# Late part of the second dense pass of a four-layer graph network: slots a block ahead, early sums added by TensorE, tables between root and norm, and the last set of blocks split

## The chip, the cores and the metric

The kernel runs on one core of a Trainium2 chip. The metric is the device time of one execution in microseconds (us). TensorE's clock has two levels, 1.2 and 2.4 GHz; the profile shows the granted clock as a share of the full one, so 0.50 is 1.2 GHz.

## The reference, cut to what matters

There are 6250 nodes with 128 features and 106,250 edges, sorted by destination: 50,000 random pairs in both directions, and one loop per node.

```python
h = relu(layernorm(x)); x = x + L0(h)   # edge weights from a small MLP, then one weighted aggregation
h = relu(layernorm(x)); x = x + L1(h)   # h = relu(conv(h, W1, b1)); h = relu(conv(h, W2, b2))
h = relu(layernorm(x)); x = x + L2(h)   # m = relu(h @ Wm1 + bm1) @ Wm2 + bm2; agg = segment_sum(m[src], dst)
                                        # h + relu([h, agg] @ Wn1 + bn1) @ Wn2 + bn2
h = relu(layernorm(x)); x = x + L3(h)   # three convs, two relus
# conv(h, W, b) = segment_sum((h @ W)[src] * dinv[src] * dinv[dst], dst) + b
```

Layer 0 has edge weights of its own. Layers 1 to 3 need six aggregations with the same graph: two in L1, one in L2, three in L3.

## The kernel before, in words

**The edge part.** The first part computes the edge weights in 220 groups of four tiles of 128 edges. For each group GpSimd (POOL) issues four gathers (`gather`, line 715). The kernel also builds a dense count matrix `adj` in device memory: 49 x 49 blocks of 128 x 128 counts in f16, one block row per window of 128 destination nodes. GpSimd adds into it with 832 scattering DMAs (`scatter`, line 723), in the order of the edges, so in the order of the destination windows. Scatters start while the gathers still run: from group 2 * BLOCKS + 12 on, every third group (those with g % 3 == 0) is followed by four scatters; the others follow when the gathers are done. Two edges of one scatter with the same place need a count of their own, so edges of a run of 1024 that fall into the same destination as the run before are put aside in "spare" rows: one more block row per set (below), with a row for each run.

**The six dense passes.** With `adj` each aggregation is a dense product: for block w, 49 matmuls (one per source chunk c) of the transposed counts `wide[c]` (128x128) with a table of the chunk in two halves, `tab` (128x256), and one last matmul that adds the spare rows by a one-hot matrix, the slot (`slots`, made by `make_slot`, line 1621; ring of two). Passes are numbered q = 0 to 5; their kinds are gcn1, message, update, gcn3, gcn3, last. `SUBS` lists the work in subs of up to seven chunks. SyncE (SP) loads pieces of `adj`, ScalarE (ACT, line 901) and in part VectorE (DVE, line 1642) widen them to f32, five subs ahead of TensorE (PE).

**Sets.** Pass 0 starts before all scatters are done. Its blocks are split into sets (`SETS`); SP waits ahead of the first piece of a set until enough scatters have landed. What a set needs is counted from the edges (`needed`): the number of edge tiles whose last edge lies below the set's end, rounded up to the next batch of 32 tiles; the last set waits for all 832. Each set begins with a unit for its spare rows (49 chunks). Behind a set stand "early" units: parts of pass 1 (kind message) over the chunks whose tables are ready. Their sums are kept in `acc`. So in pass 1 the blocks 0 to 42 are "late" units with seven chunks left (42 to 48), and the blocks 43 to 48 are "whole" units with 49 chunks.

**A late block of pass 1.** After the last matmul VectorE sums the two halves out of PSUM (`reduce_sum`, line 1521; it waits for `merged`, and in `take_sums` also for `d_turned`, that is, until TensorE has transposed the source of the block before, since the buffer `source` is written again), adds the early sum `acc` (line 1569), scales and adds the bias (1570), adds relu of it to x (1572), takes the statistics (1507 to 1509), waits for the square root on ScalarE (874), inverts it (1512) and writes the norm to `source` (1513). TensorE transposes it (`turn_source`, 1120), multiplies it up (`up`, 1131) and down (`down`, 1140) in the iterations after, and VectorE writes the table of a block three further back (`set_table`: 1598, 1525, 1526). The order on every engine is fixed by loops over `SUBS` (`TURN`, `UP` and `DOWN` say how many subs later a step comes). On VectorE an iteration is: take the sums of the block that ended, set the table of an older one, make the slot of the block that starts, casts. A late block has one sub, so one iteration is one block.

Of the kernel before, what the change touches and what calls it, by code (L numbers as in the profile page):

```python
# [7 lines left out]
D = 128  # L8
# [36 lines left out]

DB = -(-N // P)

SETS = ((0, 22), (22, 29), (29, 36), (36, 43), (43, 49))
EARLIER = len(SETS) - 1
SPARE = DB  # L50
BLOCKS = DB + len(SETS)
# [22 lines left out]


EARLY = [[(0, 22, 0, 21)], [(22, 29, 0, 21), (0, 29, 21, 28)], [(29, 36, 0, 28), (0, 36, 28, 35)],
         [(36, 43, 0, 35), (0, 43, 35, 42)], []]
UNITS = []
for n, (w0, w1) in enumerate(SETS):
    UNITS += [(0, SPARE + n, 0, DB, "spare")] + [(0, w, 0, DB, "whole") for w in range(w0, w1)]  # L80
# [11 lines left out]
def block_of(u):  # L92
    return UNITS[u][:2] if 0 <= u < len(UNITS) and UNITS[u][4] in ("whole", "late") else None


SUBS = []
# [38 lines left out]
def after(eng, sem, value):  # L135

    if value > 0:
        eng.wait_ge(sem, value)
# [10 lines left out]
def build(nc, a, out):  # L149
# [14 lines left out]
    with ExitStack() as ctx, ExitStack() as early:  # L164
# [375 lines left out]
        def spares(u):  # L540
            return sum(unit[4] == "spare" for unit in UNITS[:u + 1])
# [380 lines left out]
        def _(pe):  # L922
# [173 lines left out]
            def add_spare(u):  # L1096
                q, w = UNITS[u][:2]
                if LAYER[q]["kind"] == "update":
                    pe.wait_ge(neg_set, 1)
                    nc.tensor.matmul(ps_sum[u % 3], neg_ident[:, :], tab[q % 2][:, w, :, :].rearrange("p t d -> p (t d)"),  # L1100
                                     start=False, stop=False)
                pe.wait_ge(spare_set, spares(u))
                pe.wait_ge(slotted, q * DB + w + 1)
                nc.tensor.matmul(ps_sum[u % 3], slots[:, (q * DB + w) % SLOT_RING, :], spare_parts[:, :, :].rearrange("p t d -> p (t d)"),  # L1104
                                 start=False, stop=True).then_inc(merged, 1)
# [54 lines left out]
        def _(dve):  # L1160
            made = [0]

            def link(instruction):

                made[0] += 1
                instruction.then_inc(prep, 1)
                dve.wait_ge(prep, made[0])
# [335 lines left out]
            link(nc.vector.memset(slots[:, :, :].bitcast(f32), 0.0))  # L1503
            nc.vector.tensor_scalar(neg_ident[:, :], ident[:, :], -1.0, None, ALU.mult).then_inc(neg_set, 1)

            def normalize_block(at, into):
                link(nc.vector.bn_stats(stats_d[:, :], at))
                link(nc.vector.bn_aggr(moments_d[:, :], stats_d[:, :]))
                nc.vector.tensor_scalar(rstd_d[:, :], moments_d[:, 1:2], EPS, None, ALU.add).then_inc(d_var, 1)
                roots[0] += 1  # L1510
                dve.wait_ge(d_root, roots[0])
                link(nc.vector.reciprocal(rstd_d[:, :], rstd_d[:, :]))
                return nc.vector.tensor_scalar(into, at, moments_d[:, 0:1], rstd_d[:, 0:1], ALU.subtract, ALU.mult)  # L1513

            def x_at(q, w):
                n = X_USES.index((q, w))
                dve.wait_ge(x_back[n % XR], 16 * (n // XR + 1))
                return x_rows[:, n % XR, :]

            def reduce_sum(u, into):  # L1520
                nc.vector.tensor_reduce(into, ps_sum[u % 3].rearrange("p (t d) -> p d t", t=HALVES), AX.X, ALU.add).then_inc(reduced, 1)  # L1521
                dve.wait_ge(reduced, u + 1)
# [32 lines left out]
            def take_sums(u):  # L1555
                q, w = UNITS[u][:2]
                kind = LAYER[q]["kind"]
                dve.wait_ge(merged, q * DB + w + 1)
                after(dve, d_turned, q * DB + w)
                inv = dinv[:, 1, w:w + 1]  # L1560
                if kind == "update":
                    reduce_sum(u, source[:, 1, :])
                elif kind == "gcn1":
                    reduce_sum(u, summed_f[:, :])
                    nc.vector.tensor_scalar(source[:, 0, :], summed_f[:, :], inv, None, ALU.mult).then_inc(sourced, 1)
                elif kind == "message":
                    reduce_sum(u, summed_f[:, :])
                    if LATE_C[w]:
                        link(nc.vector.tensor_tensor(summed_f[:, :], summed_f[:, :], acc[:, w, :], ALU.add))
                    link(nc.vector.scalar_tensor_tensor(norm_d[:, :], summed_f[:, :], inv, b_row["L1_gnn_b2"][:, :], ALU.mult, ALU.add))  # L1570
                    at = x_at(q, w)
                    link(nc.vector.scalar_tensor_tensor(at, norm_d[:, :], 0.0, at, ALU.max, ALU.add))
                    after(dve, acc_set, w)
                    normalize_block(at, source[:, 0, :]).then_inc(sourced, 1)
                else:
                    reduce_sum(u, source[:, 0, :])

            def set_table(q, w):
                one = LAYER[q]
                kind = one["kind"]  # L1580
                n = q * DB + w
                dve.wait_ge(d_multiplied, n + 1)
                inv = dinv[:, 1, w:w + 1]
                if n == 0:
                    dve.wait_ge(x_stored, 16 * MC)
                if kind == "last":
                    dve.wait_ge(x_new, DB + w)
                else:
                    after(dve, tabled, n)

                def taken(instruction):
                    instruction.then_inc(d_taken, 1)
                    dve.wait_ge(d_taken, n + 1)

                if kind == "gcn1":
                    taken(nc.vector.tensor_scalar(table_d[:, :], ps_down, inv, None, ALU.mult))
                elif kind == "message":
                    taken(nc.vector.tensor_tensor(table_d[:, :], ps_down, b_row["L2_gnn_bm2"][:, :], ALU.add))
                elif kind == "update":
                    at = x_at(q, w)  # L1600
                    taken(nc.vector.tensor_tensor(at, at, ps_down, ALU.add))
                    link(nc.vector.tensor_tensor(at, at, b_row["L2_gnn_bn2"][:, :], ALU.add))
                    dve.wait_ge(acc_set, w + 1)
                    link(nc.vector.tensor_tensor(at, at, acc[:, w, :], ALU.add))
                    normalize_block(at, norm_d[:, :]).then_inc(x_new, 1)
                    dve.wait_ge(x_new, w + 1)
                    link(nc.vector.tensor_scalar(table_d[:, :], norm_d[:, :], 0.0, inv, ALU.max, ALU.mult))
                elif kind == "gcn3":
                    taken(nc.vector.scalar_tensor_tensor(norm_d[:, :], ps_down, inv, one["b"][:, :], ALU.mult, ALU.add))
                    link(nc.vector.tensor_scalar(table_d[:, :], norm_d[:, :], 0.0, inv, ALU.max, ALU.mult))  # L1610
                else:
                    at = x_at(q, w)
                    taken(nc.vector.scalar_tensor_tensor(norm_d[:, :], ps_down, inv, one["b"][:, :], ALU.mult, ALU.add))
                    nc.vector.tensor_tensor(at, at, norm_d[:, :], ALU.add).then_inc(x_new, 1)  # L1614
                    return
                split(table_d[:, :], tab[(q + 1) % 2][:, w], tabled)

            def make_slot(q, w):
                k = q * DB + w
                after(dve, merged, k - SLOT_RING + 1)  # L1620
                nc.vector.tensor_scalar(slots[0:SLOTS, k % SLOT_RING, :], window_iota_b[0:SLOTS, :], carry_of[0:SLOTS, w:w + 1], None,
                                        ALU.is_equal).then_inc(slotted, 1)

            def take(u):
                if block_of(u):
                    take_sums(u)
                elif UNITS[u][4] == "spare":
                    take_spare(u)
                else:
                    take_early(u)  # L1630

            combining = {PIECE_LAST[n]: n for n in SPARE_PIECES}
            for t in range(len(SUBS) + 1):
                if t > 0 and END[SUBS[t - 1][0]] == t - 1:
                    take(SUBS[t - 1][0])
                for u in DOWN.get(t - 1, ()):
                    set_table(*block_of(u))
                if t < len(SUBS) and START[SUBS[t][0]] == t and block_of(SUBS[t][0]):
                    make_slot(*block_of(SUBS[t][0]))
                if t + LEAD < len(SUBS) and BY_DVE[t + LEAD]:  # L1640
                    to, of = cast(dve, t + LEAD)
                    nc.vector.tensor_copy(to, of).then_inc(cast_dve, 1)  # L1642
                for at in range(t + LEAD if t else 0, t + LEAD + 1):
                    if at in combining:
                        combine(combining[at])
# [17 lines left out]
```

## Time and profile before

| | us |
|---|---|
| median of 3 runs (lowest, highest) | 4618.47 (4614.93, 4619.36) |
| the profiled execution | 4620.76 |
| its span from the first to the last instruction | 4619.0 |
| TensorE busy / VectorE busy / ScalarE busy / GpSimd busy | 3135.2 / 2544.8 / 2090.6 / 2409.5 |

The profile divides the span into 40 slices of 115.5 us. The dense passes begin at about 2256 us; pass 0 with the early units of pass 1 goes to about 3020 us, the late part of pass 1 from 3028 to 3228 us, its whole blocks to about 3285 us, and passes 2 to 5 take the rest. All times below are us from the start of the span.

### The profile page before, as it was taken

What the parts mean: (1) busy time and instruction counts of PE and PEld (TensorE: products, weight loads), DVE (VectorE), ACT (ScalarE), POOL (GpSimd) and SP (SyncE); (2) the same over time, 40 slices, a digit from 0 to 9 for tenths busy, and PEclk for the clock granted to TensorE, in tenths of its full rate; (3) what the DMA queues carried; (4) which work ended last, traced back from release to release, by engine and by line L of the source; (5) the groups of instructions that cost most, each with busy time, mean ns of one, the idle gap of its engine ahead of it and who ended that gap; (6) DMA issues with size and microseconds to landing.
All of it is one profiled execution on the core that took longest, in us unless ns stands there. A gap on an engine that the chain in (4) does not pass through costs nothing.

```text
span 4619.0 us, 87785 instructions
## 1 busy us (share of the span) xinstructions
PE 3135.2 (68%) x26574; PEld 2902.8 (63%) x26574; DVE 2544.8 (55%) x11537; ACT 2090.6 (45%) x3947; POOL 2409.5 (52%) x2044
## 2 busy tenths in 40 slices
PE   3444444433333356666799658566999999999999
PEld 3333333222222245565799648565999999999999
DVE  6555555443444479998522322367666655555544
ACT  1112211111111135555799648444555566666665
POOL 3566666777777788888888888512133200000111
PEclk8555555555555579999899879787999999999999
DMA  4888888554555579997799758522666677777787
GB/s 123 288 300 289 301 292 289 150 133 121 139 126 130 134 168 234 233 233 179 168 237 242 170 112 220 141 86 84 209 227 228 222 254 255 244 256 253 257 278 230
DMA packets 628149, 951.44 MB, mean 206 GB/s; under 512 B 192587, under 2 KB 450482, under 8 KB 622705
## 3 DMA queue, kind: packets, MB, share of 16 engines
q1 hardware_dynamic: 451248, 837.03, 56.3%
q0 software_dynamic: 171904, 107.02, 14.6%
q8 instruction: 233, 3.82, 0.3%
q10 hardware_dynamic: 4544, 1.77, 0.2%
q14 instruction: 220, 1.79, 0.1%
HBM read 752.84 MB, written 192.71 MB: 205 GB/s over the span
## 4 chain that ended last, share of the span: by engine, by line
POOL 33%; PE 32%; issue 15%; another core or an unknown queue 8%; DVE 6%; DMA 4%; ACT 1%; SPq 0%; POOLq 0%; ACTq 0%; DVEq 0%
PE ps L1091 27%; POOL adj L723 24%; POOL rows L715 9%; DMA adj<-count,place 3%; PE ps L1131 1%; PE ps L1104 1%; PE ps L1143 1%; PE ps L1140 1%; DVE same L1335 1%; DVE summed_f L1521 0%; ACT gelu L808 0%; ACT tanh_half L813 0%; DVE norm_d L1570 0%; DVE onehot_b L1363 0%
## 5 line engine op out<-in xcount | busy, mean ns | idle before, releaser
L1091 PE MATMUL ps<-tab,wide 128*128 128x256 f32 x14896 | 1950.3, 289 | 177.8 <-DVE summed_f L1521 154.9
L1091 PEld LDWEIGHTS ps<-tab,wide 128*128 128x128 f32 x14896 | 1851.7, 193 | 185.3 <-DVE summed_f L1521 159.4
L901 ACT CAST wide<-pieces 128x896 fp32r<-128x896 f16 x1466 | 1318.2, 939 | 576.9 <-PE ps L1091 393.7
L723 POOL DMA_INDIRECT adj<-count,place x832 | 1313.3, 1578 | 259.1 <-issue 245.2
L715 POOL DMA_INDIRECT rows<-table,src_of x880 | 844.2, 959 | 493.0 <-issue 247.2
L1011 PE MATMUL ps<-dst_mlp,onehot_t 128*128 x2640 | 365.1, 232 | 721.0 <-ACT onehot_t L803 392.4
L1011 PEld LDWEIGHTS ps<-dst_mlp,onehot_t 128*128 128x128 bf16 x2640 | 274.8, 104 | 801.2 <-issue 742.2
L803 ACT COPY onehot_t<-ps 128x512 bf16<-128x512 bf16 x220 | 128.9, 586 | 1307.4 <-remote 1131.7
L1642 DVE CAST wide<-pieces 128x896 fp32r<-128x896 f16 x627 | 383.1, 624 | 312.3 <-PE ps L1091 258.6
L757 POOL DMA_DIRECT2D out<-x_rows x49 | 27.4, 559 | 888.4 <-DVE x_rows L1614 880.6
L836 ACT ACTIVATE onehot<-plain,norm 128x128 f32<-128x128 bf16 x880 | 280.9, 390 | 227.9 <-DVE norm L1441 126.0
L755 POOL DMA_DIRECT2D x_list<-x_rows x98 | 53.5, 546 | 537.0 <-DVE source L1513 267.3
L1371 DVE TENSOR_TENSOR pre<-ps,rows 128x256 f32<-128x256 f32 x220 | 92.3, 420 | 375.2 <-remote 368.4
L1335 DVE SCALAR_TENSOR_TENSOR same<-spare_sum,key,ps 128x128 bf16<-128x128 f32 x832 | 281.2, 339 | 8.2 <-DMA spare_sum<-key_list 5.9
L1025 PE MATMUL ps<-weight_parts,onehot_b 128*128 128x4 bf16 x880 | 132.2, 184 | 206.2 <-DVE weight_parts L1398 99.0
L1025 PEld LDWEIGHTS ps<-weight_parts,onehot_b 128*128 128x128 bf16 x880 | 91.5, 104 | 281.8 <-issue 259.6
L1521 DVE TENSOR_REDUCE summed_f<-ps 128x128 f32<-128x256 f32 x216 | 91.7, 424 | 315.5 <-PE ps L1104 196.4
L1043 PE MATMUL ps<-rows,onehot 128*128 128x128 f32 x1760 | 261.6, 294 | 2.2 <-ACT onehot L836 2.2
L1521 DVE TENSOR_REDUCE source<-ps 128x128 f32<-128x256 f32 x196 | 83.4, 425 | 270.7 <-PE ps L1104 270.7
L1034 PE MATMUL ps<-inv_parts,low_t 128*128 128x49 bf16 x2640 | 108.8, 188 | 175.9 <-DVE low_t L1427 112.4
L1043 PEld LDWEIGHTS ps<-rows,onehot 128*128 128x128 f32 x1760 | 223.8, 199 | 2.7 <-ACT onehot L836 2.7
L1034 PEld LDWEIGHTS ps<-inv_parts,low_t 128*128 128x128 bf16 x2640 | 85.7, 98 | 215.4 <-DVE low_t L1427 126.8
(255 smaller groups left out, 3971.4 us busy)
## 6 DMA issues: line engine op xcount, KB each, us to landing
pieces<-adj SPq DMA_DIRECT2D x533, 448.0 KB
pieces<-adj SPq DMA_DIRECT2D x292, 672.0 KB
h_rows<-rows SPq DMA_DIRECT2D x220, 256.0 KB
rows<-h_rows SPq DMA_DIRECT2D x220, 256.0 KB
spare_sum<-key_list SPq DMA_DIRECT2D x104, 512.0 KB
pieces<-adj SPq DMA_DIRECT2D x151, 224.0 KB
onehot_list<-onehot_b SPq DMA_DIRECT2D x220, 128.0 KB
low_row<-low_list SPq DMA_DIRECT2D x220, 128.0 KB
```

What stands on the lines that cost most here:

```text
L715: nc.gpsimd.indirect_dma_start(out=rows_0[:, g % RING, s, :], out_offset=None, in_=table[:, :], in_offset=bass.IndirectOffsetOnAxis(ap=src ...
L723: nc.gpsimd.indirect_dma_start(out=adj[:, :], out_offset=bass.IndirectOffsetOnAxis(ap=place[:, k:k + 1], axis=0), in_=count16[:, k:k + 1], ...
L836: last = nc.scalar.activation(onehot[:, g % SUMS, s, :], plain[:, g % KEPT, s, :], ACT.Copy, scale=norm[:, g % NORMS, s:s + 1])
L901: nc.scalar.copy(to, of).then_inc(cast_act, 1)
L1011: last = nc.tensor.matmul(ps_mlp[:, g % 2, s, :], onehot_t[:, g % 2, s, :], dst_mlp[:, bass.ds(window[s], 1), part, :].rearrange("p o m -> ...
L1025: last = nc.tensor.matmul(ps_deg[:, bass.ds(window[s] * (PARTS + 1), PARTS + 1)], onehot_b[:, g % HELD, s, :], weight_parts[:, g % 2, s, : ...
L1034: last = nc.tensor.matmul(ps_inv[:, g % 2, s, :], low_t[:, g % 2, s, :], inv_parts[:, part, :], start=part == 0, stop=part == PARTS - 1)
L1043: last = nc.tensor.matmul(products[:, g % SUMS, s, :], onehot[:, g % SUMS, s, :], rows[:, g % RING, s, :], start=True, stop=True)
L1091: last = nc.tensor.matmul(ps_sum[u % 3], wide[:, t % SUB_RING, c - c0, :], tab[q % 2][:, c, :, :].rearrange("p t d -> p (t d)"), start=(c ...
L1335: nc.vector.scalar_tensor_tensor(same[r % 2][:, 0:1, :], key_row[:, n % KEYS, r:r + 1, :], key[:, t:t + 1], ps_weight[:, CROSS - 1:CROSS, ...
L1521: nc.vector.tensor_reduce(into, ps_sum[u % 3].rearrange("p (t d) -> p d t", t=HALVES), AX.X, ALU.add).then_inc(reduced, 1)
L1642: nc.vector.tensor_copy(to, of).then_inc(cast_dve, 1)
```

## The change

Four edits:

1. `SETS` has six sets in place of five: the last one, blocks 43 to 48, becomes 43 to 46 and 47 to 48. Behind the new fifth set stand early units for blocks 43 to 46 over chunks 0 to 41. So those four blocks are late units in pass 1. There is one more spare unit in pass 0, one more block row of `adj` to be cleared, `BLOCKS` is 55 in place of 54, and the first scatter follows group 123 (before: group 120).
2. In a late block TensorE adds the early sum with a matmul by the identity, f32, 128 columns; VectorE's add of `acc` is gone.
3. VectorE's part for the norm is cut in two: `measure_block` (statistics, variance out) stands at the end of `take_sums`, and `normalize_block` (wait for the root, reciprocal, norm) in `take_norm`, which comes after the older block's table.
4. The slot is made a block ahead: at the start of a block VectorE makes the slot of the next one, before it takes the sums of the block that ended.

```diff
-SETS = ((0, 22), (22, 29), (29, 36), (36, 43), (43, 49))
+SETS = ((0, 22), (22, 29), (29, 36), (36, 43), (43, 47), (47, 49))
-         [(36, 43, 0, 35), (0, 43, 35, 42)], []]
+         [(36, 43, 0, 35), (0, 43, 35, 42)], [(43, 47, 0, 42)], []]
...
                 pe.wait_ge(spare_set, spares(u))
+                if LAYER[q]["kind"] == "message" and LATE_C[w]:
+                    nc.tensor.matmul(ps_sum[u % 3][:, 0:D], ident[:, :], acc[:, w, :], start=False, stop=False)
                 pe.wait_ge(slotted, q * DB + w + 1)
...
-            def normalize_block(at, into):
+            def measure_block(at):
                 link(nc.vector.bn_stats(stats_d[:, :], at))
                 link(nc.vector.bn_aggr(moments_d[:, :], stats_d[:, :]))
                 nc.vector.tensor_scalar(rstd_d[:, :], moments_d[:, 1:2], EPS, None, ALU.add).then_inc(d_var, 1)
+
+            def normalize_block(at, into):
                 roots[0] += 1
                 dve.wait_ge(d_root, roots[0])
...
                     reduce_sum(u, summed_f[:, :])
-                    if LATE_C[w]:
-                        link(nc.vector.tensor_tensor(summed_f[:, :], summed_f[:, :], acc[:, w, :], ALU.add))
...
-                    after(dve, acc_set, w)
-                    normalize_block(at, source[:, 0, :]).then_inc(sourced, 1)
+                    measure_block(at)
...
+            def take_norm(u):
+                if block_of(u) and LAYER[UNITS[u][0]]["kind"] == "message":
+                    q, w = block_of(u)
+                    after(dve, acc_set, w)
+                    normalize_block(x_at(q, w), source[:, 0, :]).then_inc(sourced, 1)
...
+            slot_units = [u for u in range(len(UNITS)) if block_of(u)]
+            make_slot(*block_of(slot_units[0]))
             for t in range(len(SUBS) + 1):
-                if t > 0 and END[SUBS[t - 1][0]] == t - 1:
-                    take(SUBS[t - 1][0])
+                ended = SUBS[t - 1][0] if t > 0 and END[SUBS[t - 1][0]] == t - 1 else None
+                if t < len(SUBS) and START[SUBS[t][0]] == t and block_of(SUBS[t][0]):
+                    next_slot = slot_units.index(SUBS[t][0]) + 1
+                    if next_slot < len(slot_units):
+                        make_slot(*block_of(slot_units[next_slot]))
+                if ended is not None:
+                    take(ended)
                 for u in DOWN.get(t - 1, ()):
                     set_table(*block_of(u))
-                if t < len(SUBS) and START[SUBS[t][0]] == t and block_of(SUBS[t][0]):
-                    make_slot(*block_of(SUBS[t][0]))
+                if ended is not None:
+                    take_norm(ended)
```

In the update pass `set_table` calls `measure_block` and `normalize_block` one after the other, as before.

## Rows read from the trace of the kernel before

**Rows 1.** The page: busy tenths in 40 slices, TensorE and GpSimd.

```profile
PE   3444444433333356666799658566999999999999
POOL 3566666777777788888888888512133200000111
```

**Rows 2.** Windows of 10 us: busy time of PE, PEld, DVE, ACT, POOL; granted clock; DMA share.

```profile
2910.00:2920.00 10.00, 3.95 (x30) 3.39 (x28) 1.43 (x4) 3.56 (x4) 8.43 (x6) 0.86 0.37 48
2930.00:2940.00 10.00, 0.00 (x0) 0.00 (x0) 0.00 (x0) 0.00 (x0) 8.48 (x6) 0.50 0.22 0
```

**Rows 3.** Line 723 alone, window 2898 to 2960: count, durations in ns, first and last start.

```profile
L723 POOL DMA_INDIRECT adj<-count,place x33: 1554/1554/1623, 2897.9 to 2957.4; - x33
```

**Rows 4.** Timeline of TensorE around the last set: start, us, operation, idle before.

```profile
2847.12 25.08 PE L1091 MATMUL ps<-tab,wide 128*128 128x256 f32 x207
...
2966.84 8.32 PE L1091 MATMUL ps<-tab,wide 128*128 128x256 f32 x49 [52.68 <-DVE summed_f L1521]
...
2988.26 0.28 PE L1104 MATMUL ps<-spare_parts,slots 128*128 128x256 f32 x1
...
2995.24 0.28 PE L1104 MATMUL ps<-spare_parts,slots 128*128 128x256 f32 x1
```

**Rows 5.** Waits of GpSimd, 100 to 850, then 850 to 1640: total us, times, longest.

```profile
POOL rows L715 <- DVE pre L1371: 151.4, 54, 9.2
...
POOL rows L715 <- DVE pre L1371: 38.7, 17, 2.8
```

**Rows 6.** The late part's ends: first sum of it (timeline of VectorE), and the adds of early sums.

```profile
3027.54 0.42 DVE L1521 TENSOR_REDUCE summed_f<-ps 128x128 f32<-128x256 f32 x1 [0.54 <-PE ps L1104]
...
L1569 DVE TENSOR_TENSOR summed_f<-summed_f,acc x43: 291/292/296, 3028.0 to 3227.8; 128x128 f32<-128x128 f32 x43
```

**Rows 7.** Timeline of one late block, full clock, VectorE's chain and TensorE's steps in it.

```profile
3126.80 0.42 DVE L1521 TENSOR_REDUCE summed_f<-ps 128x128 f32<-128x256 f32 x1 [0.72 <-PE ps L1120]
...
3127.26 0.30 DVE L1569 TENSOR_TENSOR summed_f<-summed_f,acc 128x128 f32<-128x128 f32 x1
...
3127.59 0.35 DVE L1570 SCALAR_TENSOR_TENSOR norm_d<-summed_f,dinv,b_L_gnn_b 128x128 f32<-128x128 f32 x1
...
3128.86 0.15 DVE L1509 TENSOR_SCALAR rstd_d<-moments_d 128x1 f32<-128x1 f32 x1
...
3129.28 0.16 DVE L1512 RECIPROCAL rstd_d<-rstd_d 128x1 f32<-128x1 f32 x1 [0.27 <-ACT rstd_d L874]
3129.48 0.35 DVE L1513 TENSOR_SCALAR source<-x_rows,moments_d,rstd_d 128x128 f32<-128x128 f32 x1
...
3129.74 0.28 DVE L1598 TENSOR_TENSOR table_d<-ps,b_L_gnn_bm 128x128 f32<-128x128 f32 x1
...
3130.53 0.28 DVE L1621 TENSOR_SCALAR slots<-window_iota_b,deg 103x128 fp32r<-103x128 bf16 x1
...
3130.96 0.36 PE L1104 MATMUL ps<-spare_parts,slots 128*128 128x256 f32 x1 [2.52 <-DVE slots L1621]
...
3131.16 0.27 PE L1120 MATMUL ps<-ident,source 128*128 128x128 f32 x1
...
3131.53 0.42 DVE L1521 TENSOR_REDUCE summed_f<-ps 128x128 f32<-128x256 f32 x1 [0.72 <-PE ps L1120]
...
3132.10 1.68 PE L1091 MATMUL ps<-tab,wide 128*128 128x256 f32 x7
```

**Rows 8.** Timeline of TensorE in a late block at half the clock.

```profile
3136.03 0.41 PE L1120 MATMUL ps<-ident,source 128*128 128x128 f32 x1
...
3137.80 1.66 PE L1091 MATMUL ps<-tab,wide 128*128 128x256 f32 x7
```

**Rows 9.** Timeline of TensorE: ends of the last two whole blocks of pass 1.

```profile
3269.28 0.28 PE L1104 MATMUL ps<-spare_parts,slots 128*128 128x256 f32 x1
...
3277.18 0.28 PE L1104 MATMUL ps<-spare_parts,slots 128*128 128x256 f32 x1
```

**Rows 10.** Window 3600 to 4600, passes 2 to 5; columns as in rows 2.

```profile
3600.00:4600.00 1000.00, 999.02 (x8388) 998.81 (x8388) 547.37 (x1377) 620.71 (x812) 73.08 (x112) 1.00 0.79 255
```

More of the change, by code:

```diff
@@ L1604, in set_table @@
                     link(nc.vector.tensor_tensor(at, at, acc[:, w, :], ALU.add))
+                    measure_block(at)
                     normalize_block(at, norm_d[:, :]).then_inc(x_new, 1)
```

## The prediction

> **What bounds the kernel now.** I read the 40 slices first [rows 1]. From slice 28 on TensorE is at nine tenths or more; in slices 22 to 27 it drops to 6, 5, 8, 5, 6, 6, while GpSimd, which issues the scatters, stays at 8 until slice 24 and then stops. So two things are to be looked at: the stalls before about 2967 us, and a stretch after it in which neither engine is full. Windows of 10 us over the first place [rows 2] show TensorE at work until about 2914, and then idle at half clock with GpSimd at 8.5 of 10: pass 0 waits for scatters. The waiting ends with the last scatter, which starts at 2957.4 [rows 3]; TensorE goes on 9.4 us later, at 2966.84 [rows 4]. The second place is the late part of pass 1: its 43 blocks run from 3027.54 to 3227.8 [rows 6], (3227.8 - 3028.0)/42 = 4.757 us each, with seven source matmuls each. The timeline of one block [rows 7] shows why: VectorE does sum, add, scale, statistics, waits for the root, norm, table, slot, and only then TensorE can do the slot's matmul, for which VectorE waits in turn. It is a chain VectorE - ScalarE - VectorE - TensorE - VectorE. In passes 2 to 5 TensorE is the bound: 999 of 1000 us [rows 10].
>
> **The split set (edit 1).** The scatters that the new fifth set needs: in the reference's edges 102,237 have a destination below 47 * 128, so 798 whole tiles, which rounds up to 25 of 26 batches, 800 of 832 scatters. The 800th is the first of the 33 in [rows 3]: it starts 59.5 us ahead of the last. With the 9.4 us from start of scatter to TensorE, blocks 43 to 46 could start at 2907. TensorE is busy with early units until 2914.2 (2966.84 less the idle 52.68 [rows 4]), so scatters no longer hold it here. From 2914.2: 1.5 us for a transition (my allowance), spare unit and four wholes at 6.98 each (the distance of two slots' matmuls [rows 4]) = 34.9, then 4 x 42 = 168 early matmuls at 25.08/207 = 0.121 us, 20.4, and 1 us of ends: 2972. By then the last scatters have landed (2957.4 + 9.4 = 2966.8), so the last set starts at 2972 in place of 2966.8: 5.2 later. It is warm: before, its first 49 matmuls took 8.32 us at a low clock against 49 x 0.121 = 5.9: -2.4. And it has four wholes less: -27.9.
>
> One side effect speaks against it. The first scatters move from behind group 120 to behind group 123, so four scatters more are left when the gathers end: 4 x 1.86 = 7.4 us. In exchange the gathers end earlier, by what GpSimd needed for those four (7.4) less what it would wait for VectorE in their place. In the mixed stretch it waits only 17 times, up to 2.8 us [rows 5], before it 151.4 us in 120 groups, 1.26 each; three groups: some 4 us. So the chain of scatters ends 4 us later (bounds 0 and 7.4), and with it each set that waits. The longer clearing (one block row of 55) is done by group 108 (one row for every two groups) beside gathers that run ahead, and costs nothing here. If it did, it would be by one 55th more of the clearing's share of the first 850 us: at most 850/55 = 15, and less than the 1.26 us that GpSimd waits in each of two groups by the nearest row: I keep 0 to 2.5.
>
> Together the first late sum comes at 3027.5 + 5.2 + 4 - 2.4 - 27.9 = 3006.4: a gain of 21.1 us.
>
> **The late block (edits 2 to 4).** I add up the new iteration on VectorE from starts in [rows 7].
> - Sum to variance: 3126.80 to 3128.86 is 2.06, less the add 3127.26 to 3127.59 (0.33): 1.73.
> - Variance to table: an instruction that waits for nothing starts about its predecessor's length later, less 0.08 (norm to table: 0.26 for one of 0.35): I take 0.15.
> - Table, cast, difference, and on to the next instruction: 3129.74 to 3130.53 = 0.79. The root takes 0.42 from variance to reciprocal and is covered by 0.15 + 0.79, so its wait is gone. Without table work (the first blocks of the part) it is not.
> - Reciprocal to norm: 0.20.
> - Norm to next sum. Here is what is late next. The slot's matmul is a block ahead now and no longer waited for, and the slot's own 0.28 lies in the gap. But the next sum waits for the transpose of the source just written (in rows 7 already the transpose ends its wait, 0.10 us after its end). Norm 0.35; weights and start on TensorE 0.22 (slot's end 3130.81 to its matmul 3130.96 is 0.15, and the transpose's own lead over its weights is about 0.1); transpose 0.27; 0.10: 0.94.
>
> Sum 3.81 us against 4.73, at full clock. TensorE has in an iteration transpose, up, down, seven sources, the added early sum and the slot. The early sum as f32 128x128 is two passes (for its two such products, `up` issues four instructions), so I estimate twice the 0.12 of a source matmul, 0.23. From slot to sources before, 3130.96 to 3132.10, 1.14; with seven sources at 0.121, 0.23 and 0.3 it is 2.5: it hides below 3.81. Behind its wait for the norm TensorE's queue holds up, down and the next block's sources; those end 3.81 - 2.5 = 1.3 us ahead of need. At half clock [rows 8]: 1.77 from transpose to sources, 1.66 for these, 0.36 for the early sum, 0.3 for the slot: 4.1, and then TensorE is the bound. Half-clock and full-clock blocks alternate before; TensorE's share of an iteration rises from (1.14 + 0.85 + 0.15)/4.73 = 45% to 2.5/3.81 = 66% at full clock, so I expect more of the full. I take 3.9; bounds 3.4 (the transpose's wait hidden) and 4.7 (no gain).
>
> The Trainium skill (TensorE: Matmul & The Clock Gate, HAM oscillation) says that gaps without work bring the engine back to half rate and each burst then starts cold. The trace agrees that the slow blocks stand behind the idle gaps; by that rule alone the shorter gaps would give full clock throughout, 3.81 a block, 4 us less in the sum.
>
> The late part: from first to last sum before 42 x 4.757 = 199.8 for 43 blocks, after 46 x 3.9 = 179.4 for 47: gain 20.4.
>
> **Whole blocks of pass 1.** Two in place of six, 7.90 us each [rows 9]: gain 31.6. Their seven-sub iterations wait for ScalarE's `hidden`, which stands behind the root, and the slot now stands ahead of the sum, so up to 0.28 more for each of the two: -0.5.
>
> **Passes 2 to 5.** The slot ahead of the sum delays the sum by 0.28 in every block; VectorE is busy 547 of 1000 us [rows 10] and the source is turned several subs later, so nothing. Bounds 0 and +0.28 x 196 = 55.
>
> **Sum.** 21.1 + 20.4 + 31.6 - 0.5 = 72.6 us less than the profiled execution's 4620.8: 4548.2. That execution was 2.3 us above the median, so on the median's scale 4618.5 - 72.6 = 4546.
>
> **Rivals.**
> - A. The forecast, late blocks at 3.75 to 4.1: 4546, own range 4534 to 4558. Chance 0.62.
> - B. Another wait takes over in the late block, with a cycle near 4.4: ScalarE does cast, source, `acc`, root and two `hidden` in a fixed order, and its root stands behind a copy that waits for TensorE. For it: two engines hang on each other; against: TensorE's transpose comes about 2 us ahead of the next variance (0.94 less 0.37, then 1.73), and copy and `acc` of some 0.3 us each fit between. 46 x 0.5 = 23 more: 4569. Chance 0.18.
> - C. Everything goes better: the transpose's wait is short, cycle 3.45, scatters not later: -21 and -4: 4521. Against it the transpose ended the wait before already. Chance 0.10.
> - D. The split does not do what it says: the fifth set waits for nearly all scatters (a batch more than counted, or pieces of it stuck behind earlier ones). Then one spare unit (7.0) and 21 us of early units come behind 2967 with all six wholes: first late sum 3027.5 + 28 + 4 = 3059.5, total gain -32 + 51.5 = 19.5: 4599. The count above speaks against it. Chance 0.05.
> - E. Slower. In passes 2 to 5 the slot ahead of the sum, with its wait for the merge, holds back VectorE's casts, and TensorE waits for them. VectorE does three of seven casts there. It would need 72.6/196 = 0.37 us in each block to undo everything; with a delay of 0.42, a whole sum's length, 4546 + 82 = 4628. Against it: 45% idle VectorE and casts five subs ahead. Chance 0.03.
> - The remaining 0.02 lies between D and no change.
>
> **Range and chances.** 4524 to 4574 holds A, most of B and some of C. Differences under 0.2% (9 us) can't be told from no change. Faster by over 0.2%: 0.95; within: 0.02; slower: 0.03.
>
> **What would show it.** TensorE shows no idle stretch between 2790 and 3000 except a few us near 2918; the last scatter starts near 2961. The late part has 47 blocks from about 3007, and `L1569` is gone. In it VectorE's sum waits for L1120, the reciprocal for nothing; the slot's matmul no longer waits for the slot. Granted clock above 0.85 there. The last whole block of pass 1 merges near 3205, and from there to the end all is as before, shifted. Wrong if the late cycle is over 4.3, if TensorE idles at 2920 to 2960, or if passes 2 to 5 get longer than before.

## The result and the profile after

| | before | after |
|---|---|---|
| median (lowest to highest), us | 4617.89 (4614.93 to 4619.36) | 4533.18 (4532.02 to 4540.75) |
| runs | 4 | 4 |
| profiled execution / its span, us | 4620.76 / 4619.0 | 4540.75 / 4539.0 |
| TensorE, VectorE, ScalarE, GpSimd busy, us | 3135.2, 2544.8, 2090.6, 2409.5 | 3120.6, 2519.7, 2114.1, 2346.8 |

The ratio on record is 0.9821, 95% interval 0.9809 to 0.9833; the medians alone give 0.9817, 84.7 us. The profiled execution of after is the slowest of its four; between the two profiles lie 80.0 us. The forecast was 72.6.

Three points of the profile split the 80 us. The first late sum comes at 3009.61 (before 3027.54 [rows 6]): -17.9. From there to the last one it is 169.15 us for 47 blocks (before 3027.54 to 3227.39, 199.85 for 43): -30.7. And from there to the last whole block's merge it is 17.69 us (before 3277.18 [rows 9] - 3227.39 = 49.79): -32.1. Together -80.7. What follows is as before: from that merge to the end of the span 1342.6 us after, 1341.8 before.

One late block of after, timeline of VectorE and TensorE (start, us, operation, idle before it); it answers to [rows 7]:

```profile
3090.05 0.42 DVE L1525 TENSOR_REDUCE summed_f<-ps 128x128 f32<-128x256 f32 x1 [0.36 <-PE ps L1122]
...
3090.51 0.35 DVE L1572 SCALAR_TENSOR_TENSOR norm_d<-summed_f,dinv,b_L_gnn_b 128x128 f32<-128x128 f32 x1
...
3091.57 0.38 PE L1104 MATMUL ps<-acc,ident 128*128 128x128 f32 x2
...
3091.71 0.36 PE L1106 MATMUL ps<-spare_parts,slots 128*128 128x256 f32 x1
3091.77 0.15 DVE L1511 TENSOR_SCALAR rstd_d<-moments_d 128x1 f32<-128x1 f32 x1
3091.85 0.29 DVE L1605 TENSOR_TENSOR table_d<-ps,b_L_gnn_bm 128x128 f32<-128x128 f32 x1
...
3092.64 0.16 DVE L1516 RECIPROCAL rstd_d<-rstd_d 128x1 f32<-128x1 f32 x1
...
3092.83 0.35 DVE L1517 TENSOR_SCALAR source<-x_rows,moments_d,rstd_d 128x128 f32<-128x128 f32 x1
3093.09 0.28 DVE L1629 TENSOR_SCALAR slots<-window_iota_b,deg 103x128 fp32r<-103x128 bf16 x1
...
3093.33 0.30 PE L1122 MATMUL ps<-ident,source 128*128 128x128 f32 x1 [1.25 <-DVE source L1517]
...
3093.74 0.42 DVE L1525 TENSOR_REDUCE summed_f<-ps 128x128 f32<-128x256 f32 x1 [0.36 <-PE ps L1122]
```

The add is gone. The reciprocal has no idle time before it: the table's three instructions stand in the root's. The slot's matmul (3091.71) reads a slot that was written a block earlier; it comes 1.4 us before VectorE writes the next slot (3093.09), and nothing waits for it. What is left on VectorE is one wait per block, 0.36 us, for the transpose of the source (L1122). The waits of the late part of after (window 3015 to 3180: total us, times, longest) say the same:

```profile
PE ps L1122 <- DVE source L1517: 54.8, 44, 1.4
...
DVE summed_f L1525 <- PE ps L1122: 15.4, 43, 0.5
...
DVE rstd_d L1516 <- ACT rstd_d L874: 0.7, 2, 0.4
```

The clock, windows of 150 us in the late part (busy PE, PEld, DVE, ACT, POOL; granted clock; DMA share, GB/s), before and after. The late part of after ends at 3179, so the last 11 us of its window are not late blocks:

```profile
3040.00:3190.00 150.00, 93.87 (x538) 87.00 (x538) 106.81 (x406) 64.32 (x188) 33.63 (x63) 0.78 0.26 78
```

```profile
3040.00:3190.00 150.00, 101.48 (x794) 94.20 (x794) 122.80 (x478) 79.68 (x236) 41.77 (x78) 1.00 0.36 108
```

TensorE has 794 matmul records in place of 538 in the same time and is granted the full clock throughout.

Around the split set, timeline of TensorE after (the second line ends where the window that was read ends, at 2935):

```profile
2915.38 4.60 PE L1091 MATMUL ps<-tab,wide 128*128 128x256 f32 x35 [1.41 <-ACT wide L901]
2923.42 11.83 PE L1091 MATMUL ps<-tab,wide 128*128 128x256 f32 x84 [3.44 <-DVE summed_f L1525]
...
2965.46 26.28 PE L1091 MATMUL ps<-tab,wide 128*128 128x256 f32 x217
```

The 52.68 us of idle [rows 4] have become 3.44. The 3.44 stand at the start of the split set, behind 1.41 a little earlier. The 217 matmuls without a gap are the 168 early ones of blocks 43 to 46 and the 49 of the last spare unit: the last set no longer waits for scatters.

### The profile page after: what moved, and what is told of

Its sections match the earlier page's. It is cut to its first block, busy times and chain, and to the rows that moved or that the text cites. A ratio compares the mean times of both kernels' runs of the same rounds, so it can differ in the third digit from the quotient of the medians.

```text
span 4539.0 us, 88025 instructions
## 1 busy us (share of the span) xinstructions
PE 3120.6 (69%) x26717; PEld 2889.1 (64%) x26717; DVE 2519.7 (56%) x11482; ACT 2114.1 (47%) x3978; POOL 2346.8 (52%) x2044
## 4 chain that ended last, share of the span: by engine, by line
PE 35%; POOL 23%; another core or an unknown queue 15%; issue 12%; DVE 7%; DMA 5%; ACT 2%; SPq 0%; ACTq 0%; POOLq 0%; DVEq 0%
PE ps L1091 29%; POOL adj L723 19%; POOL rows L715 5%; DMA adj<-count,place 4%; PE ps L1133 1%; DMA pieces<-adj 1%; PE ps L1011 1%; PE ps L1145 1%; ACT wide L901 1%; PE ps L1142 1%; ACT gelu L808 1%; DVE same L1337 1%; ACT tanh_half L813 1%; PE ps L1002 1%
## 5 line engine op out<-in xcount | busy, mean ns | idle before, releaser
L901 ACT CAST wide<-pieces 128x896 fp32r<-128x896 f16 x1497 | 1344.1, 938 | 525.3 <-PE ps L1091 382.0
L1657 DVE CAST wide<-pieces 128x896 fp32r<-128x896 f16 x603 | 368.6, 624 | 250.1 <-PE ps L1091 249.1
L1629 DVE TENSOR_SCALAR slots<-window_iota_b,deg 103x128 fp32r<-103x128 bf16 x294 | 85.7, 291 | 483.4 <-PE ps L1106 447.9
L1437 DVE SCALAR_TENSOR_TENSOR inv_all<-chunk_iota,chunk_of,ps 128x49 f32<-128x49 f32 x880 | 180.7, 260 | 2.2 <-issue 1.0
```

What stands on the lines that cost most here:

```text
L901: nc.scalar.copy(to, of).then_inc(cast_act, 1)
L1437: last = nc.vector.scalar_tensor_tensor(inv_all[:, s, :], chunk_iota[:, 0, :], chunk_of[:, k:k + 1], ps_inv[:, j, s, :], ALU.is_equal, ALU ...
```

## The experiments

The kernels ran in three sets, each on one chip with the kernel before; its median was 4638.33, 4618.16 and 4637.51 us, so ratios are compared, not times. In pass 0 the same code varies from execution to execution: within the second set, where the four kernels have the same edge part, the last scatter starts at 2955.0, 2958.3, 2953.1 and 2966.3 us. That is a spread of 13 us, so I take some 5 us of every difference of medians as uncertain (an estimate). The late cycle, read in each trace, does not depend on it. Where no mean is named, it is the distance of two sums in the steady stretch; the mean over the whole late part can differ by some hundredths, since the first blocks are shorter and a few are longer. The yardstick, the changed kernel in the second set:

> The changed kernel itself, as the yardstick for the runs beside it on this chip: late cycle 3.68 us, 0.982 of before.

4533.31 us, ratio 0.9816 (0.9799 to 0.9832).

**1. The split alone.**

```diff
-SETS = ((0, 22), (22, 29), (29, 36), (36, 43), (43, 49))
+SETS = ((0, 22), (22, 29), (29, 36), (36, 43), (43, 47), (47, 49))
-         [(36, 43, 0, 35), (0, 43, 35, 42)], []]
+         [(36, 43, 0, 35), (0, 43, 35, 42)], [(43, 47, 0, 42)], []]
```

> The kernel before with only the last set split (edit 1): 43 to 46 and 47 to 48, with the early units behind it; the late block is as before. Theory (the two halves of the change are separate and each does its own part): first late sum near 3009.6 as after the change, 47 late blocks at 4.757 us, two whole blocks; against before -18 (start), +19 (46 against 42 cycles), -31: about -30, 4588 us. Rival 1 (the split gains nothing by itself, since four late blocks at 4.76 and one more spare unit and four early units cost what four whole blocks cost): within 5 us of before. Rival 2 (the split is worth more, since the idle time before the last scatter is filled with 57 us of work): -50 or more.

4604.93 us, ratio 0.9931 (0.9914 to 0.9947), -33.4 us. Late cycle 4.76 on the mean, as before, clock 0.79 in the late part. The theory holds, both rivals are out.

**2. The late block alone** (the changed kernel with the old five sets).

> The changed kernel with the old five sets (edits 2 to 4 alone). Theory: 43 late blocks at 3.68 us in place of 4.757, wholes as before: 42 x 1.08 = -45 us, 4573. With the split alone at -30 the two leave 42 - 38 = 4 cycles x 1.08 = 4 us to the sum of -80 as their product. Rival (TensorE's clock gave the gain: only with the split is TensorE warm when the late part begins): late cycle over 4.0 with alternating clock, -32 or less.

4591.55 us, ratio 0.9900 (0.9883 to 0.9916), -46.8 us, late cycle 3.68, clock 0.99 in the late part:

```profile
3040.00:3190.00 150.00, 99.27 (x758) 91.59 (x756) 122.34 (x479) 79.88 (x235) 41.91 (x78) 0.99 0.36 107
```

So the split is not what keeps TensorE at full clock there. The two alone give -80.2; both together -84.7 in their own set. The missing 4.5 us fit what four blocks more gain by the shorter cycle, 4 x 1.08 = 4.3, but they are smaller than the intervals (0.0016 of 4638, 7 us), so the times alone do not show them.

**3. Each of the three edits of the late block undone.**

Early sum on VectorE again (`matmul(..., ident, acc[:, w])` out, the add back in):

> The changed kernel without edit 2: VectorE adds the early sum again. Theory (VectorE's chain is the cycle): 0.33 comes back, cycle 4.01, 15 us slower than the changed kernel, 0.985 of before. Rival (TensorE's wait and this add overlap, since the sum waits for TensorE's transpose anyway): cycle 3.7 and 0.982.

4570.13 us, ratio 0.9854 (0.9837 to 0.9870). The timeline of VectorE with TensorE's transpose, and the clock:

```profile
3100.18 0.42 DVE L1523 TENSOR_REDUCE summed_f<-ps 128x128 f32<-128x256 f32 x1 [0.36 <-PE ps L1120]
3100.64 0.29 DVE L1571 TENSOR_TENSOR summed_f<-summed_f,acc 128x128 f32<-128x128 f32 x1
...
3103.79 0.30 PE L1120 MATMUL ps<-ident,source 128*128 128x128 f32 x1 [1.81 <-DVE source L1515]
3104.20 0.42 DVE L1523 TENSOR_REDUCE summed_f<-ps 128x128 f32<-128x256 f32 x1 [0.36 <-PE ps L1120]
```

```profile
3040.00:3190.00 150.00, 99.08 (x632) 91.04 (x631) 123.82 (x482) 75.61 (x223) 39.74 (x74) 0.84 0.33 98
```

4.02 us a cycle, 0.33 more: the add's full price. The wait for the transpose is the same 0.36, so it hides nothing of the add. The clock alternates again, 0.84.

The slot for the block that starts, behind the norm:

```diff
-            make_slot(*block_of(slot_units[0]))
...
-                if t < len(SUBS) and START[SUBS[t][0]] == t and block_of(SUBS[t][0]):
-                    next_slot = slot_units.index(SUBS[t][0]) + 1
-                    if next_slot < len(slot_units):
-                        make_slot(*block_of(slot_units[next_slot]))
...
                 if ended is not None:
                     take_norm(ended)
+                if t < len(SUBS) and START[SUBS[t][0]] == t and block_of(SUBS[t][0]):
+                    make_slot(*block_of(SUBS[t][0]))
```

> The changed kernel without edit 4: the slot is made for the block that starts, behind the norm. Theory: norm to slot 0.26, slot to next sum 1.00 over TensorE as before, 1.26 in place of 0.91: cycle 4.03, 16 us slower than the changed kernel. Rival (the slot's matmul hides behind the transpose's wait, which stands in the same gap): cycle 3.7, no difference.

4552.93 us, ratio 0.9848 (0.9830 to 0.9866), cycle 3.98 (sums at 3089.61 and 3093.59), idle before the sum 0.66. Slower by 0.30 a block, 14 us. The ratios differ by 0.0032, 15 us; the medians by 19.6. The profiled executions are 24.6 us apart, and there 11.8 stand already at the first late sum (3010.59 against 2998.84), behind scatters that end 11.3 later (2966.3 against 2955.0). So making the slot a block ahead was worth 0.30, less than the 0.72 of idle that it seemed to remove, since the transpose's wait stood right behind it.

The norm before the table:

```diff
                     measure_block(at)
+                    take_norm(u)
...
-                if ended is not None:
-                    take_norm(ended)
```

> The changed kernel without edit 3: the norm follows the root at once and the older block's table comes after it; slot ahead and early sum on TensorE stay. Theory (the transpose is late next): the table work then covers the transpose's wait in place of the root's. Cycle: sum to variance 1.72, root 0.42, to norm 0.20, norm to table 0.26, table 0.79, slot to sum 0.20: 3.59 against 3.68, so 4 us FASTER than the changed kernel. Rival (each of the three edits takes off its own wait; the root's 0.27 of idle comes back): cycle 3.95, 12 us slower.

4537.14 us, ratio 0.9819 (0.9803 to 0.9836), no difference to the changed kernel. VectorE:

```profile
3090.68 0.15 DVE L1511 TENSOR_SCALAR rstd_d<-moments_d 128x1 f32<-128x1 f32 x1
3091.20 0.16 DVE L1516 RECIPROCAL rstd_d<-rstd_d 128x1 f32<-128x1 f32 x1 [0.37 <-ACT rstd_d L874]
3091.40 0.35 DVE L1517 TENSOR_SCALAR source<-x_rows,moments_d,rstd_d 128x128 f32<-128x128 f32 x1
3091.66 0.28 DVE L1606 TENSOR_TENSOR table_d<-ps,b_L_gnn_bm 128x128 f32<-128x128 f32 x1
...
3092.45 0.28 DVE L1630 TENSOR_SCALAR slots<-window_iota_b,deg 103x128 fp32r<-103x128 bf16 x1
3092.65 0.42 DVE L1525 TENSOR_REDUCE summed_f<-ps 128x128 f32<-128x256 f32 x1
```

The wait for the root is back (0.37), and the wait for the transpose is gone: the table covers one or the other. The cycle is 3.67. The expectation had 3.59, because it took 0.42 from variance to reciprocal [rows 7]; here it is 0.52. The root ends 0.13 ahead of the reciprocal, 0.10 more than before; two more semaphore waits stand between them in this order of the code, but that they are the reason was not tried, and with a third one (`wait_at_norm_no_table` below) it is 0.52 as well. Edit 3 is worth nothing in this change, not 0.27 a block and not -0.09.

**4. What is late next: the wait for the transpose, moved.** In pass 1 `source` is written by the norm only, not by the sum.

```diff
-                after(dve, d_turned, q * DB + w)
+                if kind != "message":
+                    after(dve, d_turned, q * DB + w)
...
             def take_norm(u):
...
+                    after(dve, d_turned, q * DB + w)
                     after(dve, acc_set, w)
```

> The changed kernel with one wait moved: in pass 1 the wait for the transposed source (d_turned) stands ahead of the norm that writes source, in place of ahead of the sum. Theory (the transpose is what is late next: the sum starts 0.91 us after the norm, 0.36 of it idle on TensorE's transpose): late cycle 3.68 - 0.36 = 3.32, 46 x 0.36 = -17 us against the changed kernel, 4516. Rival (the loop over TensorE takes the place: with 2.5 us of TensorE work behind the transpose, or ScalarE's order, the cycle stays above 3.55): -6 or less.

4534.59 us, ratio 0.9776 (0.9759 to 0.9792), against 0.9821 and 0.9816 of the changed kernel, and 0.9808 of the changed kernel in this set with the first scatters behind group 120 (experiment 5). That is 0.0032 to 0.0045, 15 to 21 us, for 46 x 0.44 = 20 by the cycle. VectorE:

```profile
3082.12 0.28 DVE L1631 TENSOR_SCALAR slots<-window_iota_b,deg 103x128 fp32r<-103x128 bf16 x1
3082.31 0.42 DVE L1525 TENSOR_REDUCE summed_f<-ps 128x128 f32<-128x256 f32 x1
...
3085.55 0.42 DVE L1525 TENSOR_REDUCE summed_f<-ps 128x128 f32<-128x256 f32 x1
```

The cycle is 3.24, 0.44 less (more than the 0.36 of idle: the sum now follows the slot by 0.19). Between 3040 and 3170 VectorE has no wait left that the profile shows; TensorE is busy 90.6 us from 3050 to 3170 (79.7 in the changed kernel), at full clock.

The same with the norm before the table:

> The same without edit 3, and with the transpose's wait moved ahead of the norm. Theory: with no wait for the transpose left, the table between root and norm would be worth its whole price: without it the cycle is 3.59 as in the run beside it, against 3.24 with it, so this kernel is 16 us slower than the one with the wait moved alone, and as fast as the run beside it. Rival (the table's place does not matter, VectorE's work is the same): cycle 3.24 to 3.3.

4531.57 us, ratio 0.9813 (0.9796 to 0.9829), cycle 3.68 (sums at 3090.49 and 3094.17). VectorE waits 0.37 for the root in it. So here edit 3 is worth 0.44 a block: its price depends on whether the other wait is still there.

**5. The place of the first scatters** (behind group 120 again: `2 * BLOCKS + 10` in place of `2 * BLOCKS + 12`).

> The changed kernel with the first scatters behind group 120 again, in place of 123. Theory: 136 scatters issued by the end of the gathers in place of 132, the last scatter starts 4 us earlier and all that follows moves with it: -4 us against the changed kernel, 4529. Rival (the later end of the scatters in the changed kernel's profile, 2963.9 against 2957.4, is chance of that execution; the sets that wait are not moved by the first scatter's place): 0 against the changed kernel, 4533.

4548.89 us, ratio 0.9808 (0.9792 to 0.9824): 0.0008 to 0.0013 below the changed kernel, inside the intervals. With the moved wait:

> The changed kernel with the transpose's wait ahead of the norm and the first scatters behind group 120. Theory: cycle 3.24 (46 x 0.44 = 20 us) and scatters 4 to 6 us earlier: 25 us less than the changed kernel, 0.976 of before. Rival (the scatters' place is worth nothing): 0.9775, the ratio that the moved wait had alone.

4535.94 us, ratio 0.9777 (0.9760 to 0.9793), the same as without it. In the traces of the first and third set the last gather starts at 1649.9, 1652.5, 1658.6 and 1657.4 with group 120 and at 1647.8, 1649.1 and 1650.9 with 123; the last scatter at 2974.3, 2973.7, 2985.2 and 2979.4 against 2976.0, 2980.3 and 2980.5. The means differ by 5.4 and 0.8 us: with 123 the gathers end earlier and the scatters hardly later. These traces are of seven kernels with five, six and seven sets, so they are not alike in everything else. The 4 us expected are neither shown nor excluded: 0.0008 to 0.0013 are 4 to 6 us, the pair with the moved wait shows none, and each interval is 7 us wide to either side.

**6. One more set,** on top of the kernel above (first scatters behind group 120, wait moved).

```diff
-SETS = ((0, 22), (22, 29), (29, 36), (36, 43), (43, 47), (47, 49))
+SETS = ((0, 22), (22, 29), (29, 36), (36, 40), (40, 43), (43, 47), (47, 49))
-         [(36, 43, 0, 35), (0, 43, 35, 42)], [(43, 47, 0, 42)], []]
+         [(36, 40, 0, 35)], [(40, 43, 0, 42), (0, 40, 35, 42)], [(43, 47, 0, 42)], []]
```

> The kernel beside it with the set 36 to 42 split as well: 36 to 39, which needs 704 scatters, and 40 to 42, which needs 736 as before; early units follow each. Theory (TensorE reaches the fifth set's blocks 16 us after their scatters, 2923 against 2907, because it is still busy with what the release at 2789 let in): with 4 blocks let in 60 us sooner, TensorE is through before 2907, and all from there comes about 12 us earlier; idle time appears at 2880 to 2907: 0.973 to 0.974 of before. Rival (one more set costs its spare unit and its clearing, and the last scatters hold back the end anyway): no gain or 5 us slower, 0.976 to 0.977.

4528.55 us, ratio 0.9761 (0.9745 to 0.9778), the lowest of all, but the interval overlaps with 0.9777 of the kernel beside it. TensorE:

```profile
2883.60 6.83 PE L1091 MATMUL ps<-tab,wide 128*128 128x256 f32 x49 [0.24 <-ACT wide L901]
2925.89 15.19 PE L1091 MATMUL ps<-tab,wide 128*128 128x256 f32 x105 [35.46 <-DVE summed_f L1525]
...
2968.77 14.51 PE L1091 MATMUL ps<-tab,wide 128*128 128x256 f32 x119
2987.73 2.47 PE L1091 MATMUL ps<-tab,wide 128*128 128x256 f32 x10 [4.46 <-ACT wide L901]
```

(The last line ends with the window, at 2990.) TensorE is through early, as expected, and idles 35.5 us; but now the last set waits for its own scatters (4.46 idle at 2987.7, the last scatter at 2979.4). In the kernel beside it the split set started at 2940.69, with the last scatter at 2985.2: against the last scatter the start is 9.0 us earlier. From the last scatter to the first late sum it is 40.4 us, against 41.7 in the kernel beside it: 1.3 us of the 12 expected. Theory and rival were each half right: the earlier release works, and the wait for the last scatters takes back most of it.

## Why the prediction was right

The forecast was 4546 (range 4524 to 4574); measured 4533. By its steps:

- **Start of the late part.** Forecast 3006.4; in the profile 3009.61. The last set began at about 2965.5 + 168 x 0.121 = 2985.8, not at 2976: the transition took 3.44 + 1.41 us in place of my 1.5, and the last scatter came at 2963.9, 6.5 after the one of before, where I had 4. But in the yardstick's profile it came at 2955.0 and the first late sum at 2998.84, 28.7 us ahead of before's 3027.54, where the forecast had 21.1. So the 4 us for the scatters' place can't be read from one profile, and experiment 5 does not show such a cost. The profile of after, 7.6 us above its median, is likely such an execution; that is inferred.
- **Late cycle.** Forecast 3.9, measured 169.15/46 = 3.68. This is the term of the sum that was mis-sized: 46 x 0.22 = 10 us. Between the medians 12 to 13 us are missing from the forecast; between the profiles 7.4, since the start fell 3.2 short there and hid part of the 10. Its full-clock working, 3.81, was close: 1.72 (forecast 1.73), 0.08 (0.15, where the prediction's own rule, 0.15 less 0.08, gives 0.07), 0.79 (0.79), 0.19 (0.20), 0.91 (0.94). The other part was the clock. I took a value between full and half clock, and it stayed full, 1.00. Why it stayed full is only in part shown. TensorE's longest idle stretch in a full-clock block fell from 2.52 us [rows 7] to 1.25, and the clock rose from 0.78 to 1.00; with 1.81 us (`add_on_vector`) it was 0.84. The Trainium skill (TensorE: Matmul & The Clock Gate, HAM oscillation) has work after a long idle gap start at half rate. This trace agrees that the clock goes with the gaps, but not on where it falls: behind the 2.52 us the slot's matmul and the transpose still took their full-clock times (0.36 and 0.27), and only the seven sources, 1.1 us later, took the half-clock 1.68 [rows 7]. So the prediction's sentence that the slow blocks stand behind the idle gaps is too simple.
- **What is late next.** The transpose, as forecast: 0.36 of idle in 44 of the 47 blocks, 15.8 us in all from 3009 to 3182, named in rival C as what keeps the cycle from 3.45. Experiment 4 shows it: with that wait moved the cycle is 3.24.
- **The three edits do not add up.** The prediction summed the iteration as a whole and so was not misled; but it counted the root's wait as gone and the transpose's as the new one without saying that they are two sides of one thing. Experiment 3 shows that edit 3 is worth nothing here beside the two others. Undone one at a time, the three edits account for 0.33, 0.00 and 0.30 of the 1.08 us that a block lost; no run undoes two of them, so how the rest is shared, and what of it is the clock's, stays open.
- **Whole blocks.** Forecast -31.1, measured -32.1.
- **Passes 2 to 5.** Forecast 0, measured +0.8 in the profile. VectorE's wait for the merge stands before the slot now and TensorE does not notice.
- **Rivals.** B (another wait, cycle 4.4) did not come: ScalarE's root waited for VectorE (41.2 us from 3015 to 3180), hardly the other way round (0.7 us). D did not come: TensorE's idle time before the split set was 3.44. E did not come.

## What to carry to other kernels

When a chain through several engines sets the cycle, put its new order on paper from start to start and look for the wait that becomes last; two covers for two waits may be one cover that only moves. Before adding cover, see what the wait protects: here it stood ahead of an instruction that does not write the buffer, and moving it (experiment 4) gave a further 0.3% to 0.45% without any new work. Blocks that wait for data in order can be cut where the data's own batches end; here one more cut (experiment 6) gained little, since the last batch held the end.

## What was not expected of the hardware

With a cycle of 4.02 us and the seven sources, up, down, transpose and slot, TensorE's clock alternated (0.84 on average, `add_on_vector`); with 3.98 us and the early sum's matmul as well it stayed at 1.00 (window 3040 to 3190 of the kernel without the slot ahead: PE 92.20 busy of 150, against 99.08 where it alternates, the slow half making the busy time longer):

```profile
3040.00:3190.00 150.00, 92.20 (x714) 84.84 (x715) 115.63 (x453) 74.57 (x225) 40.86 (x76) 1.00 0.32 95
```

The two f32 instructions that the change adds to TensorE may be what kept its clock up, but that is not shown: the slot also stands elsewhere in these two kernels, and TensorE's longest idle stretch in a steady full-clock block is 1.81 us in one and 1.54 in the other. At 4 us a cycle the clock mattered little for the time, since VectorE set it: in `add_on_vector` a cycle in which the clock fell (3047.21 to 3051.37, granted 0.60) took 4.16, the next one, at 0.57, 4.01, and the mean over the late part is 4.04.
